# Mamba front of a fused attention and scan kernel: convolution taps and softplus sums moved to GpSimd, z gated from PSUM, side work in other slots, residual loaded early

## What is computed

```python
xm, z = jnp.split(h @ W_in, 2, axis=-1)            # 512 channels each
xc = causal_depthwise_conv(xm, conv_w, 4 taps) + conv_b
xm = silu(xc)
dtr, Bm, Cm = jnp.split(xm @ W_xp, [64, 80], axis=-1)
dt = softplus(dtr @ W_dt + b_dt)
def step(hst, inp):                                 # 64 steps, state 512 x 16
    dA = exp(dt_t[:, :, None] * A)
    hst = hst * dA + (dt_t * x_t)[:, :, None] * B_t[:, None, :]
    y = einsum('bds,bs->bd', hst, C_t)
y = (ys + xm * D_param) * silu(z)
out = residual + gate * (y @ W_out)                 # rows put back in order
```

## Time and profile before

| what | us |
|---|---|
| median of 3 executions (2619.96 to 2621.88) | 2620.96 |
| the profiled execution, its own time | 2619.73 |
| its span, first to last instruction | 2618.0 |
| busy: TensorE matmul, weight load | 2286.5, 1698.1 |
| busy: VectorE, ScalarE, GpSimd | 2208.3, 1612.2, 1053.9 |
| from the first gather of y to the end of the span | 139.1 |
| mean of a decay (L589), a scaling on GpSimd (L436) | 0.495, 0.73 to 0.75 |

### The profile page before, as it was taken

How to read it: one execution, slowest core, us unless ns; L and a number is a source line. 1 busy time by engine, 2 the same in 40 slices (tenths; PEclk the granted TensorE clock), 3 DMA queues, 4 the chain that set the end, 5 groups by cost and what they waited for, 6 DMA issues and landing times. The chain is left out here.

```text
span 2618.0 us, 45310 instructions
## 1 busy us (share of the span) xinstructions
PE 2286.5 (87%) x14265; PEld 1698.1 (65%) x14265; DVE 2208.3 (84%) x4358; ACT 1612.2 (62%) x3396; POOL 1053.9 (40%) x1404
## 2 busy tenths in 40 slices
PE   5999999999967999999999999999999999998600
PEld 3666666666635777767777777677777776777500
DVE  3888888888846999999999999999999999999711
ACT  1222222222237888879888888798888887988400
POOL 1222222222224645556446455564464545635200
PEclk9999999999978999999999999999999999999955
DMA  3111111111100000000000000000000000000065
GB/s 107 43 43 43 43 44 47 46 43 43 40 29 9 8 11 14 9 13 14 5 17 5 14 13 9 14 13 5 17 5 13 13 9 13 5 5 9 23 181 190
DMA packets 71046, 80.42 MB, mean 31 GB/s; under 512 B 12182, under 2 KB 63193, under 8 KB 68762
## 3 DMA queue, kind: packets, MB, share of 16 engines
q1 hardware_dynamic: 70810, 77.52, 9.5%
HBM read 43.94 MB, written 33.55 MB: 30 GB/s over the span
## 5 line engine op out<-in xcount | busy, mean ns | idle before, releaser
L589 ACT ACTIVATE decay<-dtT,decay_rate 128x256 f32<-128x256 f32 x2048 | 869.3, 495 | 0.2
L485 PE MATMUL bank<-ident,decay 128*128 128x128 f32 x4096 | 622.9, 275 | 113.9 <-DVE fresh L704 39.5
L495 PEld LDWEIGHTS bank<-ident,scaled 128*128 128x128 f32 x4096 | 485.4, 142 | 233.7 <-issue 199.2
L495 PE MATMUL bank<-ident,scaled 128*128 128x128 f32 x4096 | 623.7, 275 | 2.1 <-POOL scaled L436 2.0
L485 PEld LDWEIGHTS bank<-ident,decay 128*128 128x128 f32 x4096 | 471.2, 141 | 159.1 <-ACT decay L589 126.5
L436 POOL TENSOR_SCALAR scaled<-state,bc 128x512 f32<-128x512 f32 x384 | 277.9, 732 | 430.4 <-DVE state L704 398.2
L436 POOL TENSOR_SCALAR scaled<-fresh,bc 128x512 f32<-128x512 f32 x384 | 285.8, 753 | 316.8 <-DVE fresh L704 257.4
L694 DVE TENSOR_TENSOR bank<-bank,fresh 128x512 f32<-128x512 f32 x512 | 338.8, 690 | 58.2 <-PE bank L485 54.9
L694 DVE TENSOR_TENSOR bank<-bank,state 128x512 f32<-128x512 f32 x512 | 334.8, 689 | 28.4 <-PE bank L485 22.5
L704 DVE SCALAR_TENSOR_TENSOR state<-dtx,bc,bank 128x512 f32<-128x512 f32 x512 | 356.6, 736 | 0.0
L704 DVE SCALAR_TENSOR_TENSOR fresh<-dtx,bc,bank 128x512 f32<-128x512 f32 x512 | 356.5, 736 | 0.0
(11 more groups left out here) (141 smaller groups left out, 3596.2 us busy)
## 6 DMA issues: line engine op xcount, KB each, us to landing
xt<-in_x_dram SPq DMA_DIRECT2D x64, 128.0 KB, 2.0
resid<-x SPq DMA_DIRECT2D x64, 128.0 KB, 2.8
normed<-xh SPq DMA_DIRECT2D x64, 128.0 KB, 1.9
xg<-normed SPq DMA_DIRECT2D x64, 128.0 KB, 2.1
ssm_out<-yo SPq DMA_DIRECT2D x32, 256.0 KB, 2.0
fin_y<-ssm_out SPq DMA_DIRECT2D x64, 128.0 KB, 2.1
fin_r<-resid SPq DMA_DIRECT2D x8, 1024.0 KB, 6.5
out_dram<-fin_r SPq DMA_DIRECT2D x8, 1024.0 KB, 8.5
```

What stands on the lines that cost most here:

```text
L485: mm = pe.transpose(dec_bank[i % DECAY_BANKS][:, m * P:(m + 1) * P], decay[:, i // BLOCK % 2, n % GROUP, m, t % HALF * P:(t % HALF + 1) * ...
L495: mm = pe.matmul(y_bank[t % HALF][:, m * P:(m + 1) * P], scaled[:, i % RING, m * P:(m + 1) * P], ident[:, :], is_transpose=True, start=Fal ...
L589: act.activation(decay[:, block % 2, e // CB, m, :], dtT[:, par, m, half * HTOK:(half + 1) * HTOK], ACT.Exp, scale=decay_rate[:, m, n:n + ...
```

## The change

The taps and the sum of softplus go to GpSimd. Each of the 12 taps becomes a product into a small buffer (`tap`, two of them) and a sum into `xs`, 24 instructions, at slots `TAP_SLOTS`, 6 to 30. max(dt, 0) is taken by ScalarE (Relu in place of Identity), GpSimd adds the logarithm and multiplies by x, alternating, in slots 48 to 55. z is no longer copied: ScalarE takes the tanh of the product in PSUM, and VectorE computes (tanh + 1) times the product in PSUM, which frees the bank. The slots of nearly all side work change, bc comes before dt, with two steps in one piece. `xs`, `dtT`, `dtx` and `zs` become two tensors each, so that the residual (8.4 MB, all 64 steps) can be loaded over the ones that the last chunk does not use. At the end SP and ScalarE each gather half of the groups, all of them before their first store.

```diff
-                "dtr dt0 dt1 dt2 dt3 bc out0 x0 x1 x2 x3").split()
+                "dtr bc dt0 dt1 dt2 dt3 out0 x0 x1 x2 x3").split()
-        SLOTS = dict(zip(JOBS, ((0,), (1,), (3, 4), (5, 6), (7, 8), (9, 10), (11, 12, 13),
-                                (14, 15), (16, 17), (18, 19), (20, 21),
-                                (22, 23, 24, 25), (27,), (29,), (31,), (33,), (35, 36, 37, 38),
-                                (42, 43, 44), (46,), (48,), (50,), (52,))))
+        SLOTS = dict(zip(JOBS, ((0,), (1,), (2, 3), (4, 5), (6, 7), (8, 9), (11, 12, 13),
+                                (14, 15), (17, 18), (21, 22), (24, 25),
+                                (32, 33, 34, 36), (37, 38), (39,), (40,), (42,), (44,),
+                                (46, 47, 48), (58,), (60,), (61,), (62,))))
-        MODULATE, CARRY, SOFTPLUS, PRODUCT, GATES = (28, 33), 24, 38, 39, 54
+        TAP_SLOTS = [6 + q * 26 // (2 * TAP_ADDS) for q in range(2 * TAP_ADDS)]
+        X_TANH, X_GATE, Z_GATE = (13, 19, 26, 32), (14, 20, 28, 34), (18, 20, 24, 28)
+        MODULATE, CARRY, SOFTPLUS = (37, 41), 34, 48
...
+            def prefetch_resid():
+                sp.wait_ge(s_state, (CHUNKS - 1) * ITEMS)
+                sp.wait_ge(s_summed, (CHUNKS - 1) * ITEMS)
+                moved(sp, CHUNKS - 2, "x3")
+                for g in range(STEPS // FIN):
+                    sp.dma_start(fin_r[:, g * FIN:(g + 1) * FIN, :], resid_seq[:, g * FIN:(g + 1) * FIN, :])\
+                        .then_inc(s_fin_r, 16)
...
+        def final_rows(eng, first):
             for q in range(2):
+                eng.wait_ge(s_y_out[q], 16 * CHUNKS + 16)
+            for g in range(first, STEPS // FIN, 2):
+                for t in range(g * FIN, (g + 1) * FIN):
+                    row = eng.value_load(order[0:1, t:t + 1], min_val=0, max_val=STEPS - 1)
+                    eng.dma_start(fin_y[:, t:t + 1, :], ssm_out[:, bass.ds(row, 1), :]).then_inc(s_fin_y[g], 16)
+            for g in range(first, STEPS // FIN, 2):
+                eng.wait_ge(s_sum, g + 1)
+                eng.dma_start(out[:, g * FIN:(g + 1) * FIN, :], fin_r[:, g * FIN:(g + 1) * FIN, :]).then_inc(s_out, 16)
...
+            def add_tap(c, par, at, step):
+                m, k = at // (TAPS - 1), at % (TAPS - 1)
+                done = (c + 1) * TAP_ADDS + at
+                x = xs[1 - par][:, m, :]
+                if step == 0:
+                    if k == 0:
+                        gp.wait_ge(s_tap0, (c + 1) * CB + m + 1)
+                    reached(gp, s_tap, done - 1)
+                    apart(gp)
+                    gp.tensor_scalar(tap[:, at % 2, :], raw[:, m, k * P:k * P + TOK], taps[:, m, k:k + 1], 1.0,
+                                     ALU.mult, ALU.mult).then_inc(s_tapmul, 1)
+                else:
+                    gp.wait_ge(s_tapmul, done + 1)
+                    reached(gp, s_tap, done)
+                    gp.tensor_tensor(x, x, tap[:, at % 2, :], ALU.add).then_inc(s_tap, 1)
+
+            def softplus_times_x(c, par, m, step):
+                v = dtT[1 - par][:, m, :]
+                if step == 0:
+                    gp.wait_ge(s_softexp, (c + 2) * (CB + 1))
+                    gp.tensor_tensor(v, v, tmp[:, m, :], ALU.add).then_inc(s_dt, 1)
+                else:
+                    gp.wait_ge(s_dt, (c + 1) * CB + m + 1)
+                    gp.tensor_tensor(tmp[:, m, :], v, xs[1 - par][:, m, :], ALU.mult).then_inc(s_dtxT, 1)
...
                 if kind == "z":
-                    ins = act.activation(zs[:, 1 - par, k, :], side[:, :], ACT.Copy)
+                    act.activation(zs[1 - par][:, k, :], side[:, :], ACT.Tanh, scale=0.5).then_inc(s_ztanh, 1)
+                    return
...
-                    act.activation(dtT[:, 1 - par, k, :], side[:, :], ACT.Identity, bias=dt_bias[:, k:k + 1])
+                    act.activation(dtT[1 - par][:, k, :], side[:, :], ACT.Relu, bias=dt_bias[:, k:k + 1])
...
+                    if pre and i in Z_GATE:
+                        k = Z_GATE.index(i)
+                        ve.wait_ge(s_ztanh, (c + 1) * CB + k + 1)
+                        b = side_turn(c, f"z{k}")[0]
+                        z = zs[1 - par][:, k, :]
+                        ve.scalar_tensor_tensor(z, z, 1.0, side_bank[b][:, :], ALU.add, ALU.mult)\
+                            .then_inc(s_side_moved[b], 1)
```

More of the change, by code:

```diff
@@ L394, in mamba_sync @@
                 body(c, c % 2, True, c < CHUNKS, c < CHUNKS - 1)
+            final_rows(sp, 0)
+            sp.wait_ge(s_out, 16 * (STEPS // FIN))
+        def final_rows(eng, first):
             for q in range(2):
[L397 to L415, removed]
+                eng.wait_ge(s_y_out[q], 16 * CHUNKS + 16)
[6 more added lines that the diff above has]
+                eng.dma_start(out[:, g * FIN:(g + 1) * FIN, :], fin_r[:, g * FIN:(g + 1) * FIN, :]).then_inc(s_out, 16)
         def mamba_gpsimd(gp):
@@ L443, in body @@
                         modulate(c + 2, MODULATE.index(i))
+                    for q in range(2 * TAP_ADDS):
+                        if pre and i == TAP_SLOTS[q]:
+                            add_tap(c, par, q // 2, q % 2)
                     if pre and i == CARRY:
-                        gp.wait_ge(s_tap, (c + 2) * 3 * CB)
+                        gp.wait_ge(s_tap, (c + 2) * TAP_ADDS)
                         apart(gp)
@@ L540, in fill @@
                     pe.wait_ge(s_xs, (c + 1) * CB + piece + 1)
-                    mm = pe.matmul(side[0:DTR, :], w_xp[:, piece, 0:DTR], xs[:, 1 - par, piece, :],
+                    mm = pe.matmul(side[0:DTR, :], w_xp[:, piece, 0:DTR], xs[1 - par][:, piece, :],
                                    start=(piece == 0), stop=(piece == CB - 1))
                 elif kind == "bc":
-                    t = piece
-                    for m in range(CB):
-                        mm = pe.matmul(side[:, t * 2 * DS:(t + 1) * 2 * DS], xs[:, 1 - par, m, t * P:(t + 1) * P],
+                    for t, m in itertools.product((2 * piece, 2 * piece + 1), range(CB)):
+                        mm = pe.matmul(side[:, t * 2 * DS:(t + 1) * 2 * DS], xs[1 - par][:, m, t * P:(t + 1) * P],
                                        w_xp[:, m, DTR:DTR + 2 * DS], start=(m == 0), stop=(m == CB - 1))
@@ L588, in make_decay @@
                     act.wait_ge(s_dt, c * CB + m + 1)
-                act.activation(decay[:, block % 2, e // CB, m, :], dtT[:, par, m, half * HTOK:(half + 1) * HTOK],
+                act.activation(decay[:, block % 2, e // CB, m, :], dtT[par][:, m, half * HTOK:(half + 1) * HTOK],
                                ACT.Exp, scale=decay_rate[:, m, n:n + 1]).then_inc(s_decay, 1)
@@ L709, in gate @@
                 if t == 0:
-                    ve.wait_ge(s_zs, (c + 1) * CB)
+                    for k in range(CB):
+                        moved(ve, c - 1, f"z{k}")
                 ve.wait_ge(s_summed, c * ITEMS + index_of(DS - 1, t) + 1)
-                z = zs[:, par, :, t * P:(t + 1) * P]
+                z = zs[par][:, :, t * P:(t + 1) * P]
                 ve.tensor_tensor(z, y_bank[t % HALF][:, :].rearrange("p (a b) -> p a b", b=P), z, ALU.mult)\
@@ L741, in body @@
                         rows(c, c - 1, 1)
[L742 removed]
+                    if scan and i == 50:
                         rows(c, c, 0)
[L744 to L751 removed]
```

106 lines of the change are left out of this document (39 added, 67 removed).

## The result

| | before | after |
|---|---|---|
| median of the runs, us | 2620.46 | 2650.06 (2641.31 to 2652.41) |
| ratio, 95% interval | | 1.0106 (1.0082 to 1.0131) |
| span of the profiled run | 2618.0 | 2646.7 (its own time 2648.45) |
| first state step | 805.50 | 824.84 |
| mean period of a chunk | 105.17 | 111.39 |

A forecast was written before the change was run, and what follows sets the result against it. TensorE and VectorE were taken as tied slot by slot, neither alone the bound. 2618.0 + 23 (15 chunks) + 14.5 (start) - 78 (end) = 2577.5, rounded to 2578; with own-time and median offsets 2581, range 2530 to 2612.

The forecast's parts named there:

- The end: From the first y gather on: two gather queues and the residual loaded early, -78 us, from -70 to -84.
- The start: Before the scan, where nothing hides GpSimd's taps and sums: +14.5 us, from +10 to +18.
- x gates priced .65 each: VectorE's slots 16 to 31: six gates, four for z and two for x, at 0.65 each, 3.9 us.
- Rival B: x gates held up by GpSimd's taps: up to 5.1 us a chunk, 2658 in all; chance 0.04.
- The walk of the chunk: Scan chunk followed from TensorE's slot 0 through both engines' stretches: 106.7 us, +1.5 a chunk.
- hT: First u piece, moved from slot 3 to 2, waits for hT: about 1.7 plus 0.3 for ScalarE, 2.0 a chunk.
- The Ln's stall: Slot 49: TensorE waits for the two decays that ScalarE makes after the Ln, 2.7 us a chunk, before 1.55.
- The x transposes: Slots 58 to 62, behind GpSimd's sums: 1.7 us late, of which the two banks' lead hides all but 0.3.
- GpSimd's "about 71": GpSimd's busy time in a chunk of the changed kernel: near 71 of 107 us.
- Rival A: The balance comes through, with no stall at the Ln or hT: chunks of 102.0, 2511 in all; chance 0.25.

The follow-up runs named there:

- end_only: Kernel before with the new end alone (tensors split by parity, residual loaded in the last chunk, y rows gathered by two queues): 2539.07 us, ratio 0.9688.
- filler: Changed kernel with dummy TensorE matmuls in front of three long waits (two in slot 29, two in slot 48, one in slot 57): 2624.81 us.
- gate22_no_filler: Changed kernel, bc behind dt, x gates in slots 22 and 32, u pieces later, softplus from slot 46, first front's taps and softplus on VectorE: 2494.66 us.
- gate_one_input: Changed kernel with an x gate that reads one SBUF operand in place of two, the product with x left out: 2634.22 us.
- gates_swapped: Changed kernel with the x gate in front of the z gate in slots 20 and 28, where both stand: 2648.95 us.
- bc_last_filler: Changed kernel with bc behind dt and dummy TensorE matmuls, two in slot 29 and two in slot 57: 2585.54 us.

## Why the prediction was wrong

- **The end** (-78): right; -82 here and in end_only. Gathers took 34.8 (forecast 34.5); what follows them 22.3, where I had 26.
- **The start** (+14.5): +19.3. I had +14.1 up to the last x gate; it ended 17.2 later, because GpSimd's sums and the gates met there too (three sums of 1.75, the last gate 1.49). From there to the Ln it was +5.9 for my +4, and the rest -3.8 for my -3.6.
- **"x gates priced .65 each"**: this step failed. Rival B, the gates held up by GpSimd's taps, was right that they meet, and I set its price by the largest gate of the trace before (0.88, a delay of 0.2), as if that were what a meeting costs. But there GpSimd was busy 12.4 of the 24.1 us in which VectorE went through slots 16 to 31 (1468.95 to 1493.08); now it is busy 22.1 of 25.7 (1517.27 to 1542.99). The gates at slots 20 and 28 took 1.54 and 1.77 on the mean, +2.0 a chunk, and it was all on the path. This is rival B at some 40% of its price (5.1), and I gave it 0.04. That the time came out near B's 2658 is luck: the clock made up the rest.
- **The clock was not in the sum at all.** The rows before had it at 1.00 and I took that as given, though I forecast new waits of 2 to 3 on TensorE. It cost 1.8 a chunk.
- **The walk of the chunk** (106.7) can be held against a chunk of filler in which the clock stayed, on TensorE and VectorE: slot 0, slot 32, the turn behind the Ln (in slot 49), VectorE's first pair of the next chunk, slot 0 again.

```profile
1042.84 0.60 PE L510 MATMUL bank<-ident,decay 128*128 128x128 f32 x4
1097.22 0.63 PE L510 MATMUL bank<-ident,decay 128*128 128x128 f32 x4 [1.96 <-DVE state L730]
1132.91 0.66 PE L510 MATMUL bank<-ident,decay 128*128 128x128 f32 x4 [0.78 <-ACT decay L621]
1151.84 1.29 DVE L720 TENSOR_TENSOR bank<-bank,state 128x512 f32<-128x512 f32 x2
1152.45 0.60 PE L510 MATMUL bank<-ident,decay 128*128 128x128 f32 x4
```

| stretch | walk | measured |
|---|---|---|
| slot 0 to slot 32 | 53.05 | 54.38 |
| slot 32 to the turn behind the Ln | 35.3 | 35.69 |
| from there to VectorE's next chunk | 18.5 | 18.93 |
| VectorE's next chunk to TensorE's slot 0 | -0.15 | 0.61 |

- The gates' 2.0 lie in the first stretch; the rest of it came out 0.7 shorter than my walk, most of that at hT, which I had at 2.0 and which waited 1.37. The Ln's stall, priced 2.7, is right: taking it away gave 109.6 to 106.9. **The x transposes were priced too low**: TensorE ends the chunk 0.6 behind VectorE, where I had it 0.15 ahead (0.45, less 0.3 for the transposes), +0.8. The two middle stretches are 0.4 each too short in my walk; what makes that is open.
- Per chunk: 1.5 forecast, 2.0 gates, 1.8 clock, 0.8 transposes, 0.8 in the middle stretches, less 0.7, make the 6.2.
- **GpSimd's "about 71"** was a slip: my own terms give 56.1 + 23.4 + 5.1 - 10.2 = 74.4, and it measures 73.9.
- **Rival A** (102.0, the balance comes through) was right about what the idea can give and wrong about these slots: 102.57 in gate22_no_filler.

The gates show the hold-up itself. In the changed kernel each of the 30 gates over 1.2 ended 0.54 to 0.57 after the end of a GpSimd instruction, 29 times a tap sum and once the carry copy. A gate as `tensor_scalar` with one SBUF operand was held too, 1.58 for 0.47 in gate_one_input. The 64 z gates, whose other operand is in PSUM, were not: 0.676 to 0.689, 0.681 on the mean, though the 45 of them in slots 18, 20 and 24 overlap a tap sum by 0.29 or more.

## What to carry to other kernels

A short hold-up seen in a trace is a sample of one alignment, not a bound (a gate took 0.88 at most before and up to 1.87 in the changed kernel): before moving work to GpSimd, list which VectorE instructions without a PSUM operand will stand in its busy stretch, here the x gates, and move those out; one gate moved from slot 28 to 32 took the period from 111.39 to 108.42. A z gate, with a PSUM operand, kept its 0.68 there. A stall of TensorE is priced by what follows it: ahead of its own dense stretch, slots 32 to 47, it may cost its length and then the clock (1.8 a chunk by filler); ahead of VectorE's stretch, at slot 50, the fall of the clock cost 0.1 to 0.2 at most. And when one change has several parts, run each alone: here the end's 82 us hid that the rest cost 111, which a few moved slots and the first front turned into a gain of 44.

## What was not expected of the hardware

- In gates_swapped a held VectorE instruction let a whole row of GpSimd instructions pass: a gate that began 0.08 behind a scaling's start took 2.42, 1.74 more than the 0.68 of one that was not held.
- The start times do not tell who goes first. In the changed kernel the gate of slot 28 begins 0.62 to 0.66 behind the start of GpSimd's scaling in all 15 chunks; 14 are held (1.83 to 1.87) and one, at 0.65, is not (0.68). It is the thirteenth in filler and bc_last_filler too; why is open. With the clock behind it this is 4 us a chunk. Runs of the changed kernel spread over 11 us and those of gate22_no_filler over 2; that the falls of the clock make the difference is not shown.
- GpSimd's copy with one operand holds a gate as well: in the first front the last gate began 0.52 after the carry copy (786.90, 1.46) and took 1.49.
- In the changed kernel the clock stayed after 12 of TensorE's 15 waits of 1.69 to 1.84 at slot 58, and fell after 8 of the 15 of 2.5 at slot 50 and 11 of the 14 of 2.9 at slot 30. In bc_last_filler it fell after 8 of 14 waits of 1.95 to 1.97.
